# Four-part value matmuls, swapped output weights, and softmax sums taken during the exponentials

## The reference, cut to what matters

```python
# L0X: 16 query heads of 64, 4 key/value heads; L3X is alike with 16 key/value heads
scores = einsum('bhqd,bhkd->bhqk', q, k) / sqrt(64)
out = einsum('bhqk,bhkd->bhqd', softmax(scores), v)
return out.reshape(B, Tq, 16 * 64) @ Wo
# L0F: self-attention with 16 heads of 8, plus a top-2 mixture of 8 experts of the same input
attn = softmax(einsum('bqhd,bkhd->bhqk', q, k) / sqrt(8))
attn_out = einsum('bhqk,bkhd->bqhd', attn, v)
gate = softmax(x @ W_gate + b_gate); combine = top-2 of gate
moe_out = einsum('bsef,bse->bsf', einsum('bsd,edf->bsef', x, W_experts) + b_experts, combine)
return attn_out + moe_out
# every layer
x = x + tanh(g) * layer(layernorm(x), ctx)
```

## Time and profile before

| | before |
|---|---|
| median of three runs | 4556.94 us |
| the profiled execution | 4552.95 us |
| its span | 4551.1 us |
| PE busy | 3947.3 us (87%) |
| DVE busy | 3006.2 us (66%) |
| ACT busy | 1735.9 us (38%) |
| POOL busy | 764.9 us (17%) |
| chain that ended last | PE 60%, DVE 18%, SP's queue 8%, issue 7%, POOL 2%, DMA 2% |
| mean granted TensorE clock | 0.866 |

### The profile page before, as it was taken

One profiled execution on the slowest core, in us unless ns is written; L12 is line 12 of the kernel. 1 busy time (PEld: TensorE's weight loads), 2 busy tenths in 40 slices (PEclk: granted clock), 3 DMA queues, 4 the chain that ended last, 5 costly groups with the idle time before them and its releaser, 6 DMA issues.

```text
span 4551.1 us, 105680 instructions
## 1 busy us (share of the span) xinstructions
PE 3947.3 (87%) x36890; PEld 3104.3 (68%) x36890; DVE 3006.2 (66%) x9082; ACT 1735.9 (38%) x4156; POOL 764.9 (17%) x575
## 2 busy tenths in 40 slices
PE   6999978888886888889999999777737899999965
PEld 4888855555554555589999999655537777777754
DVE  4666657777775777766666666799861355555569
ACT  3555534444442344333333333222203344444421
POOL 1222221111110000011111111100171122222211
PEclk9999987777776677689999999888758999999975
DMA  3000010000001000000000000100015200000000
GB/s 124 8 7 8 7 23 6 6 6 6 6 7 65 16 16 15 15 6 0 0 0 0 0 0 3 44 12 12 6 39 191 98 12 12 9 12 12 10 13 26
DMA packets 102053, 97.04 MB, mean 21 GB/s; under 512 B 31664, under 2 KB 91056, under 8 KB 101296
## 3 DMA queue, kind: packets, MB, share of 16 engines
q1 hardware_dynamic: 97408, 76.94, 5.6%
q0 software_dynamic: 4096, 8.40, 0.6%
q10 hardware_dynamic: 432, 10.19, 0.6%
HBM read 46.97 MB, written 19.66 MB: 15 GB/s over the span
## 4 chain that ended last, share of the span: by engine, by line
PE 60%; DVE 18%; SPq 8%; issue 7%; POOL 2%; DMA 2%; ACT 1%; DVEq 1%; POOLq 0%; ACTq 0%
PE ps L768 54%; SPq L591 7%; PE ps L936 5%; DVE acc L1658 2%; DMA arena_a<-kT 1%; DVE o_sb L1637 1%; POOL scr L718 1%; PE ps L806 1%; DVE arena_b L1606 1%; POOL route L740 1%; DVE xn L1442 1%; DVE x_sb L1557 1%; DVE st L1401 1%; DVE mx L1527 1%; DVE vsmall L1614 1%
## 5 line engine op out<-in xcount | busy, mean ns | idle before, releaser
L768 PE MATMUL ps<-xcT,small 128*128 128x256 f32 x2176 | 610.1, 419 | 34.7 <-DMA xcT<-in_ctxT 25.4
L732 POOL TENSOR_TENSOR rstd<-veps,neghalf 128x2 f32<-128x2 f32 (+1 forms) x224 | 167.9, 749 | 2403.8 <-DVE veps L1434 2071.2
L768 PEld LDWEIGHTS ps<-xcT,small 128*128 128x128 f32 x2176 | 411.3, 204 | 233.3 <-issue 114.5
L768 PE MATMUL ps<-arena_b,qT 64*64 64x64 f32 (+3 forms) x11136 | 541.8, 242 | 21.6 <-DVE arena_b L1606 20.3
L1278 ACT ACTIVATE kT<-ps 128x256 f32<-128x256 f32 (+1 forms) x768 | 294.4, 383 | 623.6 <-PE ps L768 547.4
L768 PE MATMUL ps<-small,xcT 128*64 128x64 f32 (+5 forms) x3072 | 482.7, 384 | 51.4 <-DVE acc L1658 30.3
L768 PE MATMUL ps<-xhi,parts_a 128*128 128x256 f32 (+1 forms) x2112 | 500.4, 289 | 22.7 <-DVE qT L1687 22.7
L768 PEld LDWEIGHTS ps<-arena_b,qT 64*64 64x64 f32 (+3 forms) x11136 | 463.5, 149 | 58.4 <-issue 35.0
L1248 ACT ACTIVATE pT<-ps 128x512 f32<-128x512 f32 (+1 forms) x576 | 303.3, 571 | 467.0 <-PE ps L936 465.3
L1687 DVE TENSOR_TENSOR qT<-kT,ps 128x256 f32<-128x256 f32 (+1 forms) x768 | 316.8, 419 | 188.5 <-ACT kT L1278 181.0
L768 PE MATMUL ps<-xlo,parts_a 128*128 128x256 f32 (+1 forms) x1536 | 430.6, 280 | 0.0
(11 more groups left out here) (212 smaller groups left out, 6388.5 us busy)
## 6 DMA issues: line engine op xcount, KB each, us to landing
wbuf<-parts_b SPq DMA_DIRECT2D x39, 512.0 KB, 3.0
arena_a<-kT SPq DMA_DIRECT2D x1024, 8.0 KB
xcT<-in_ctxT SPq DMA_DIRECT2D x96, 128.0 KB, 2.1
xn<-scr SPq DMA_DIRECT2D x39, 128.0 KB, 2.2
scr_y<-acc SPq DMA_DIRECT2D x39, 128.0 KB, 2.9
scr<-vsmall SPq DMA_DIRECT2D x9, 512.0 KB, 13.3
ctx_sb<-in_ctx SPq DMA_DIRECT2D x32, 128.0 KB, 2.1
arena_a<-in_w ACTq DMA_DIRECT2D x1, 4096.0 KB, 12.4
```

Of the source, the lines that this page charges most:

```text
L732: pool.tensor_tensor(rstd[:, 0:n], veps[:, 0:n], neghalf[:, 0:n], ALU.pow).then_inc(s_rstd.sem, 1)
L768: return nc.tensor.matmul(o, lhsT, rhs, start=start, stop=stop, skip_group_check=True)
```

## The change

Three things change.

1. Stage A of L0X and L3X runs in four parts of the array. The two sequences of a tile now go to different column halves: part (row half, column half = row half XOR hb). The result of row half 0 lands in one bank, that of half 1 in the other. The second sequence's results therefore stand on swapped partitions. ACT copies each bank with two instructions over 64 partitions instead of one over 128.
2. Stage W of L0X and L3X is split by sequence: 16 matmuls of 128x64x128 instead of 8 of 128x128x128. The first sequence uses `Wo` as before, the second a copy whose upper and lower half are swapped. SP loads this copy twice, with two DMAs of 64x1024 each: once at the start, between the first weights and the bulk of x, and once in the sixth layer in front of its first tile. PE's start of L0X waits for it.
3. In L0F the exponentials also give their sums (`accum_out`). DVE takes reciprocals of them in N0 and N1, which now stand behind V0 (before, nothing was there), GpSimd multiplies the probabilities in place, and stage T waits for that. Stage A reads 16 value columns per pair of heads instead of 18, and DVE adds attention and experts in one step and updates the residual once.

```diff
-        s_probs = step("s_probs", l0x=2, l3x=2)
+        s_probs = step("s_probs", l0x=2, l0f=2, l3x=2)
+        wo_swapped = arena_b[:, 6144:7168]
@@ SP @@
+            def swap_wo(src, a, b):
+                for half in range(2):
+                    sp.dma_start(wo_swapped[half * S:(half + 1) * S, :],
+                                 src[(1 - half) * S:(2 - half) * S, a:b]).then_inc(s_swap, 16)
             sp.dma_start(small[:, 0:FIRST_W], small_in[:, 0:FIRST_W]).then_inc(s_small, 16)
+            swap_wo(small_in, *SMALL_AT["l0x_wo"])
             sp.dma_start(x_sb[:, n:NT, :], x_v[:, n:NT, :]).then_inc(s_x, 16)
...
                 sp.wait_ge(s_lo, 16)
+                a = LATE.index("l3x_wo") * 1024
+                swap_wo(late_in, a, a + 1024)
                 load_tile(0)
@@ POOL @@
-                if item[0] == "N" and layer in (L0X, L3X):
+                if item[0] == "N" and layer in (L0X, L0F, L3X):
@@ PE, start @@
                     pe.wait_ge(s_small, 16)
+                    pe.wait_ge(s_swap, 32)
@@ PE, heads_times_values @@
-                for turn in ((0, 1), (1, 0)):
-                    halves = (0, 1) if turn == (0, 1) else (1, 0)
-                    for i, hb in blocks:
-                        for half in halves:
...
+                n = 2 if layer is L0X else 8
+                for c, half, hb in itertools.product(range(n), range(2), range(2)):
+                    rows = slice(half * S, (half + 1) * S)
+                    to = slice((half ^ hb) * S, ((half ^ hb) + 1) * S)
+                    w0, heads = 512 // n, 8 // n
+                    last = mm(bank(banks[half])[to, c * w0:(c + 1) * w0],
+                              v_heads(layer, g.par)[rows, 2 * t + hb, c, :],
+                              pT[rows, t, c * heads:(c + 1) * heads, hb * S:(hb + 1) * S])
+                    if (c, hb) == (n - 1, 1):
+                        last.then_inc(filled[banks[half]], 1)
@@ PE, T, A and W @@
-                    if layer in (L0X, L3X):
+                    if layer in (L0X, L0F, L3X):
                         pe.wait_ge(s_probs.sem, s_probs.after(g, t))
-                    elif layer is L0F:
-                        wait_drained(layer.score_ring, g, t)
...
-                                last = mm(o[:, c * 36:(c + 1) * 36], pT[:, t, c, :],
-                                          v_small(g.par)[:, 2 * t:2 * t + 2, c, :])
+                                e = 16 if layer is L0F else 18
+                                last = mm(o[:, c * 2 * e:(c + 1) * 2 * e], pT[:, t, c, :],
+                                          v_small(g.par)[:, 2 * t:2 * t + 2, c, 0:e])
...
+                    if chunks == 8:
+                        for c in range(8):
+                            for hb in range(2):
+                                toks = slice(hb * S, (hb + 1) * S)
+                                wo = w(layer.name + "_wo") if hb == 0 else wo_swapped
+                                last = mm(bank(b)[toks, 0:D], oT[:, t, c, toks], wo[:, c * D:(c + 1) * D],
+                                          start=c == 0, stop=c == 7)
@@ ACT, P in L0F and A in L0X, L3X @@
+                    act.wait_ge(s_rv.sem, s_rv.after(g.back(1), t))
...
-                                                    bias=negmax[:, t, h:h + 1], scale=layer.scale)
+                                                    bias=negmax[:, t, h:h + 1], scale=layer.scale,
+                                                    accum_out=sm[:, t, h:h + 1])
...
-                        nc.scalar.activation(o, i, ACT.Copy).then_inc(drained[b], 1)
+                        for hb in range(2):
+                            rows = slice((j ^ hb) * S, ((j ^ hb) + 1) * S)
+                            last = nc.scalar.activation(oT[rows, t, :, hb * S:(hb + 1) * S],
+                                                        bank(b)[rows, :].rearrange("p (c q) -> p c q", q=S), ACT.Copy)
+                        last.then_inc(drained[b], 1)
@@ DVE, N and A in L0F @@
+                if layer is L0F:
+                    wait_drained(layer.score_ring, g, t)
+                    dve.reciprocal(rv[:, t, 0:nh], sm[:, t, 0:nh]).then_inc(s_rv.sem, 1)
                     return
...
+                    if layer is L0F:
+                        src = bank(b, c * 2 * e).rearrange("p (c b e) -> p c b e", b=2, e=e)
+                        wait_drained(fr, g, layer.use(("Z", t)))
+                        for half in range(2):
+                            rows = slice(half * S, (half + 1) * S)
+                            last = dve.tensor_tensor(o_sb[rows, t, :].rearrange("p (c e) -> p c e", e=e),
+                                                     src[rows, :, half, :],
+                                                     acc[rows, g.par, t, :].rearrange("p (c e) -> p c e", e=e), ALU.add)
+                        last.then_inc(drained[b], 1)
+                        wait_drained(ring, g, u)
+                        residual(layer, g, t, o_sb[:, t, :]).then_inc(s_upd.sem, 1)
+                        return
...
-                    if layer is L0F:
-                        wait_drained(fr, g, layer.use(("Z", t)))
-                        residual(layer, g, t, acc[:, g.par, t, :])
```

More of the change, by code:

```diff
@@ L12 @@
+import itertools
 from contextlib import ExitStack
@@ L783, in start @@
                     pe.wait_ge(s_late, 16)
+                    pe.wait_ge(s_swap, 64)
                     pe.wait_ge(m_out, TILES2)
@@ L860, in heads_times_values @@
                 pe.sem_inc(s_ready, 1)
-                blocks = [(0, hb) for hb in range(2)] if layer is L0X else [(i, hb) for i in range(4) for hb in range(2)]
-                for turn in ((0, 1), (1, 0)):
-                    halves = (0, 1) if turn == (0, 1) else (1, 0)
-                    for i, hb in blocks:
-                        for half in halves:
-                            j = turn[half]
-                            rows = slice(half * S, (half + 1) * S)
-                            if layer is L0X:
-                                last = mm(bank(banks[j])[rows, hb * 256:(hb + 1) * 256],
-                                          v_heads(layer, g.par)[rows, 2 * t + hb, j, :],
-                                          pT[rows, t, 4 * j:4 * j + 4, hb * S:(hb + 1) * S])
-                            else:
-                                last = mm(bank(banks[j])[rows, i * P + hb * S:i * P + (hb + 1) * S],
-                                          v_heads(layer, g.par)[rows, 2 * t + hb, 4 * j + i, :],
-                                          pT[rows, t, 4 * j + i, hb * S:(hb + 1) * S])
-                            if turn == (1, 0) and (i, hb) == blocks[-1]:
-                                last.then_inc(filled[banks[j]], 1)
+                n = 2 if layer is L0X else 8
[8 more added lines that the diff above has]
+                        last.then_inc(filled[banks[half]], 1)
             def do(layer, item, g):
@@ L1641, in do @@
                     last.then_inc(drained[b], 1)
-                    if layer is L0F:
-                        wait_drained(ring, g, u)
-                        residual(layer, g, t, o_sb[:, t, :]).then_inc(s_upd.sem, 1)
                 elif kind == "E":
```

12 lines of the change are left out of this document (5 added, 7 removed).

## The result

The changed kernel takes 4497.25 us (median of four runs, 4495.28 to 4498.92), the kernel before 4559.17 in the same comparison (4556.47 to 4561.93): ratio 0.9864, 95% interval [0.9847, 0.9881]. The prediction said 4539: -18 us was forecast and -62 measured. The profiled execution took 4495.28, with a span of 4493.3 (before 4551.1, so -57.8) and a mean granted clock of 0.863 (before 0.866).

A forecast was written before the change was run, and what follows sets the result against it. PE was taken to bound L0X and L3X, a chain through several engines L0F. The terms -21 - 45 + 0 + 4 + 44 = -18 us against 4552.95 gave 4535, as a median 4539 us; range 4475 to 4605.

The forecast's parts named there:

- Stage A in L0X (-21): Four-part value matmuls in L0X: nothing gained at A0, 0.66 us left per group at A1, 21 us saved over 32 groups.
- Stage A in L3X (-45): Four-part value matmuls in L3X: 2 x 0.92 us saved less a new wait of 0.43 per group, 45 us saved.
- Stage W (0): Halved output projection in L0X and L3X: sixteen halves last as long as eight full matmuls, 0 us; upper bound 29 us.
- 16h + t: Length of a stage W block: sixteen half-matmul intervals h of 0.108 us and one tail t of 0.23, together 1.95 us.
- DMAs (+4): Loads of the swapped output weights: 1.5 us more at the start and 2.5 in the sixth layer, together 4 us.
- L0F, the sums on ACT (+44): Sums taken with L0F's exponentials on ACT: 24.23 us per pass, 1.42 more than before, +44 us over 31 passes.
- The ring: L0F's loop of waits: exponentials, C's copy, Z0, E1.0, next exponentials; 19.43 + 32x us, predicted to set the period.
- x: Price of one sum beside an exponential on ACT in L0F: 0.15 us taken, bounds 0 and 0.39.
- rival 1: Sums on ACT in L0F nearly free, below 0.106 us each: -76 us, 4481 us; chance 0.25.
- L0F, DVE (-14): DVE's shorter stage A in L0F: 0.45 us less from A1 to V0, nothing at A0, 14 us over 31 passes.
- L0F, GpSimd: GpSimd's two multiplications in L0F, 1.90 us each: just hidden behind PE's work before T1.
- Rival 4: ACT's copies out of PSUM take all of stage A's gain in L0X and L3X: 0 instead of -66, 4605 us; chance 0.06.

## Why the prediction was wrong

By its own steps:

- **Stage A in L0X (-21), right, but not the whole of what was changed there.** The loop went from 17.66 to 17.21, -0.45 per group. With W's +0.27 taken out, stage A gives -0.72, against 0.66 predicted. The waits are where it put them (`xcT` before Q0, four copies before A1).
- **Stage A in L3X (-45), right.** -1.36 per group against -1.41 (-1.28 with W's -0.08 taken out), the wait 0.49 against 0.43. The loop as a whole gave 38.9 us, since its first passes are shorter and gain less. Four copies take 2.27 us, not 2.05: 0.485 per further copy was worked out from two copies on two banks, and the 64-partition ones follow each other every 0.56.
- **Stage W (0), mis-sized.** +0.135 per stage in L0X, -0.04 in L3X, +4.5 us over the kernel. The prediction's bounds (0 to 0.23 per stage) held it in the mean. Setting 16h + t by another stage's block left out what a change of width does beside its neighbours.
- **DMAs (+4).** They cost 2 at the start (1.5 said); in the sixth layer nothing that can be told from its own spread of 8 us.
- **L0F, the sums on ACT (+44): the step that failed.** The ring was taken to bind, and it does not: its price is 0. The term that made it bind is x, 0.15 instead of the measured 0.09: 32 times 0.06 is 1.9 us per pass, and with 0.09 the prediction's own sum is 22.3, below the period of 22.8. That is rival 1. The 0.15 took the 64 elements off the distance of two exponentials and let the read-out cost the rest; in the trace it takes less. The estimate that the prediction took from the Trainium skill ("ScalarE: Activation LUTs", section "What ACT_TABLE_LOAD costs"), 0.093 us per read-out, agrees with the 0.09 of the trace. A second term was mis-sized too: the way from E1.0 to the exponentials was read off one pass (11.40) and set against a mean period over all passes; its mean before is 10.9. With both put right the ring is slack by about 1 us.
- **The ring where it does bind.** Three added copies make x = 0.139 in effect. The ring then has 23.9 us per pass, and 23.5 was measured; L0F has 703.5 us, 14 more than before, where the prediction's sum has +33. That this kernel as a whole stands 29 us below the one before, and that -62 + 33 is -29 too, is luck: the prediction's other terms sum to -62, and the first and seventh layers' part measured alone gave -39.7.
- **L0F, DVE (-14), too small.** It was 24 us in fact. The way from A1 to V0 is 0.37 us shorter (0.45 said). The copy at A0 alone costs nothing, so that step stands; but A0 and A1 together move the mix of long and short passes, which no sum of single durations has.
- **L0F, GpSimd:** hidden, right by 0.2 us.
- **Left out:** the ends of L0X and L3X, +4.3 and +2.8 us, where a wait that other work hides in the loop is bare, and the granted clock is down behind it.
- **Rival 4 (the copies out of PSUM take all):** they took a part. Of 2 x 0.92 us per group in L3X 1.28 is left, of 2 x 0.79 in L0X 0.72.
- **Two readings without weight:** DVE is busy 57 to 61% in L0X and L3X, not 53 to 61. The second line of the earlier trace rows is the last but one power (the last starts at 1336.37); it is 30 distances from the first, so the mean of 22.81 stands.

Put together, the prediction with x = 0.09 was its own rival 1, 4481 us. The measured 4497 lies 16 above it: W has 5 of that, the two ends 7, and the rest is the balance of smaller gains in the two loops and a larger one in L0F.

## What to carry to other kernels

Before a ring (a loop of waits through several engines) is set against a period, take each of its legs as a mean over the passes, or all of them from the same pass: where the clock changes from pass to pass, a leg from one pass can miss the mean (by 0.5 us here). What decided here was the price of an instruction that no row showed; such a term is worth its bounds before a sum is built on one value of it. When a copy on ScalarE is split in two along partitions, count both at full price (587 ns against 594 here), and look in the code for stages that can stand between producer and consumer; here that order was worth another 31 to 35 us. Before moving a stage, check which PSUM bank it takes, who has to empty it, and which waits the program ties to a stage's place in the order and not to what it reads.

## What was not expected of the hardware

- An `accum_out` on ScalarE shows as a second instruction. It costs 0.09 us in a chain of 64-element exponentials (0.201 apart without, 0.290 with), though its records are 312 ns long.
- Eight fp32 matmuls of 128x128x128 split into sixteen of 128x64x128 cost 0.135 us per stage among blocks of full width and nothing (-0.04) among blocks of half width. By the starts, 0.1 to 0.2 us goes where a block of one width stands beside one of the other.
- 0.43 us more on VectorE per pass cost 0 at one place, 8.5 us at another, and 22 at both: with both, more of the passes were the long kind, 23.5 us instead of 21.1, in which the granted clock is 0.50 to 0.65 where a short one has 0.62 to 1.00.
